# Norms of the queries: the two halves added on VectorE, and the exponential's table loaded earlier

## The chip, the core and the metric

The kernel runs on one core of one Trainium2 chip. The metric is the device time of one execution in microseconds (us); the median of several is taken. TensorE (PE), VectorE (DVE), ScalarE (ACT) and GpSimd (POOL) each work through a list of instructions of their own and wait for one another on semaphores; SyncE (SP) issues most of the transfers.

## What is computed

Four stages over x (8 batches of 256 tokens, width 256): a cross-attention to sets, a mixture of 16 experts with a shared one, a second cross-attention, and a second mixture of 8 experts. The change lies in the second cross-attention, of which this is the part that matters (with 256 image tokens only the image keys count):

```
x = x + L0_xattn(layernorm(x));  x = x + L0_ffn(layernorm(x))
def rms_norm(x, g, eps=1e-6):
    var = mean(x * x, axis=-1);  return x * rsqrt(var + eps) * g
q = rms_norm(layernorm(x) @ Wq + bq, gq)       # var: one number per token, over 256 columns
k_img = rms_norm(ctx_img @ Wk_img + bk_img, gk_img)
img_x = softmax(q k_img / 4) v_img             # 16 heads of 16 columns
x = x + img_x @ Wo + bo
x = x + L1_ffn(layernorm(x))
```

## The kernel before

The second cross-attention has two parts. In the first, the queries of all 8 batches are made; `queries(b)` and `squares(b)` are one batch of it. In the second, 16 tiles of 128 tokens (`NT`) go one by one through scores, maximum, exponential, transposition, values, division and projection.

Queries are kept transposed: the 256 columns of a query lie as two halves (`m` = 0, 1 of `KD` = 2) of 128 partitions, and the 256 tokens of a batch along the free axis. For each batch:

- PE, `queries(b)` (L1136): four fp32 matmuls 128x128 by 256 columns into one PSUM bank. In the trace each fp32 matmul is two records, so a batch is 8.
- ACT, `queries(b)` (L823, L825): for each half, a Square into `sqT` (in `arena`, two buffers and `sqT_last` for batch 7), then an Identity into `xnT`, which is the query itself; both add the bias. Semaphores `c_sq` and `c_qT` count them.
- PE, `squares(b)` (L1144): the squares are summed over the partitions, by matmuls of `sqT` with one column of ones. For each of the two tiles of a batch the halves `m` = 0 and 1 are accumulated in PSUM: four matmuls of one column, 8 records. `c_ssq` counts them, and ACT waits for it before it writes a buffer of `sqT` again.
- DVE, `mean_squares(half)` (L1620), for four batches at once, scales the sums; POOL raises them to -1/2 (L610, `rq`, semaphore `c_rq`), and the exponential takes `rq` as its scale.

The order on each engine is the order of the code. PE runs q0, the bias product of the output (L1157, L1158), the last piece of the first mixture's down projection, q1, s0, then q2, s1, q3, s2, q4, s3 (q for queries, s for squares), the transpositions of the normalised rows of batches 6 and 7 (L933, `turn_rows`), q5, s4, q6, s5, the scores of tile 0 (L1180), q7, s6, s7, the scores of tile 1, the transposition of tile 0's probabilities (L1189), values (L1202, L1209), and so on. The transposition of batch 7 takes its PSUM bank after ACT has copied batch 6 out of one (`copy_batch`, L711).

ACT runs q0, `bo_rows` (the output's bias, L829), q1 to q4, `preload_act_table(Exp)` (L832), the copies of batches 6 and 7, q5 to q7, and then the exponential of tile 0 (L846), which waits for `rq`, for tile 0's scores less their maximum (`c_shift`) and for s6.

DVE, after the first mixture, adds its last group to x (L1578), takes the statistics of batches 6 and 7 (L1384 to L1394) and their rows (`rows_of`, L1405), then `mean_squares(0)`, the maxima of tile 0 (L1626), its centring (L1634) and `mean_squares(1)`.

POOL meanwhile makes the block-diagonal keys (L588), adds the output's bias to x (L604, 8 instructions), and then makes `rq` (L610).

Of the kernel before, what the change touches and what calls it, by code (L numbers as in the profile page):

```python
# [14 lines left out]
ALU = mybir.AluOpType  # L15
ACT = mybir.ActivationFunctionType
AX = mybir.AxisListType

P = 128
B, S, D = 8, 256, 256  # L20
# [38 lines left out]
def program(nc, x_in, ctx_in, ctxT_in, itok_in, descT_in, wq0_in, bq0_in, rw0_in, ebias_in,  # L59
            gu0_in, dn0_in, wq1_in, bq1_in, gq1_in, wk1_in, bk1_in, gk1_in, wv1_in, bv1_in,  # L60
            wo1_in, bo1_in, wg1_in, wexp_in, out_rows):
    with ExitStack() as st:
# [3 lines left out]
        def sem(name):  # L66
            return st.enter_context(nc.semaphore(name))
# [35 lines left out]
        def view(tensor, first, *shape):  # L103
            v = tensor[:, first:first + int(np.prod(shape))]
            names = "abcd"[:len(shape)]
            if len(shape) > 1:
                v = v.rearrange(f"p ({' '.join(names)}) -> p {' '.join(names)}",
                                **dict(zip(names[:-1], shape)))
            return v
# [67 lines left out]
        sqT = view(arena, 1024, 2, KD, S)  # L177
        sqT_last = view(arena, 3072, KD, S)
        attT = view(wexp, last + 1280, 2, KD * P)
        rec1 = view(arena, 3840, P)  # L180
        attU = view(wexp, last + 1024, KD * P)
        srep1 = view(arena, 4096, P)
# [86 lines left out]
        def bank(i, n=1):  # L269
            return ps[:, 512 * i:512 * (i + n)]  # L270
# [22 lines left out]
        c_proj, c_pv, c_q, c_qT = sem("c_proj"), sem("c_pv"), sem("c_q"), sem("c_qT")  # L293
        c_rec, c_rq, c_scores = sem("c_rec"), sem("c_rq"), sem("c_scores")
        c_shift, c_sq, c_ssq, c_turned = sem("c_shift"), sem("c_sq"), sem("c_ssq"), sem("c_turned")
        c_var = sem("c_var")

        d_added, d_down, d_hT = sem("d_added"), sem("d_down"), sem("d_hT")
        d_hidden, d_logits, d_max, d_onehot = sem("d_hidden"), sem("d_logits"), sem("d_max"), sem("d_onehot")
# [52 lines left out]
        def each(eng, n, lead, step, body):  # L352


            for i in range(lead):
                body(i, i)
            with eng.Fori(0, (n - lead) // step) as turn:
                for j in range(step):
                    body(turn * step + (lead + j), lead + j)
# [347 lines left out]
        def _(act):  # L707
# [110 lines left out]
            def queries(b, k):  # L818
                act.wait_ge(c_q, b + 1)
                if k >= 2:  # L820
                    act.wait_ge(c_ssq, b - 1)
                for m in range(KD):
                    act.activation(sqT_last[:, m, :] if k == B - 1 else sqT[:, k % 2, m, :], bank(3 - k % 2)[:, m * S:(m + 1) * S], ACT.Square,  # L823
                                   bias=vecs[:, 0, m:m + 1]).then_inc(c_sq, 1)
                    act.activation(xnT[:, m, bass.ds(b * S, S)], bank(3 - k % 2)[:, m * S:(m + 1) * S],  # L825
                                   ACT.Identity, bias=vecs[:, 0, m:m + 1]).then_inc(c_qT, 1)
            queries(0, 0)
            act.wait_ge(bo_sum, 1)
            act.activation(bo_rows, bank(4)[:, 0:D], ACT.Copy).then_inc(bo_ready, 1)  # L829
            for b in range(1, 5):  # L830
                queries(b, b)
            act.preload_act_table(ACT.Exp)  # L832
            for b in range(B - 2, B):
                copy_batch(2, b, 0)
            for b in range(5, B):
# [83 lines left out]
        def _(pe):  # L919
# [218 lines left out]
                mm.then_inc(c_q, 1)  # L1138

            def squares(b, k):  # L1140
                pe.wait_ge(c_sq, b * KD + KD)
                for j in range(TB):
                    for m in range(KD):
                        mm = pe.matmul(bank(7 - b // 4)[:, b % 4 * TB + j:b % 4 * TB + j + 1], (sqT_last if k == B - 1 else sqT[:, k % 2])[:, m, j * P:(j + 1) * P],  # L1144
                                       ones[:, 0:1], start=(m == 0), stop=(m == KD - 1))
                mm.then_inc(c_ssq, 1)

            def queries_squares(b, k):
# [229 lines left out]
        def _(dve):  # L1378
# [18 lines left out]
            def rows_of(norm, b, k):  # L1397

                dve.wait_ge(ln_rstd, norm * B + b + 1)
                if k >= 2 or norm >= 2:  # L1400
                    dve.wait_ge(ln_turned, norm * B + b - 1)
                for j in range(TB):
                    t = b * TB + j
                    to = xn_of[norm]
                    r = dve.tensor_scalar(to[:, k % 2, j, :], x_sb[:, t, :], mean[:, bass.ds(t, 1)],  # L1405
                                          rstd[:, bass.ds(t, 1)], ALU.subtract, ALU.mult)
                r.then_inc(ln_rows, 1)
# [165 lines left out]
            def add_ffn0(g):  # L1573
                dve.wait_ge(b_down, g * C0 + C0)
                for j in range(2):
                    t = g * 4 + j * 2
                    o = x_sb[:, bass.ds(t, 2), :].rearrange("p t d -> p (t d)")
                    dve.tensor_tensor(o, o, bank(6 + j), ALU.add).then_inc(x_new, 1)  # L1578

            def ffn0_group(g, k):  # L1580
                if k:
                    add_ffn0(g - 1)
                for c in range(C0):
# [22 lines left out]
                    if k and c in (5, 7):  # L1606
                        rows_of(2, g * 2 - 2 + (c - 5) // 2, (c - 5) // 2)
            each(dve, NG, 1, 1, ffn0_group)
            add_ffn0(NG - 1)
            dve.wait_ge(x_new, XB)  # L1610
            for b in range(B - 2, B):
                stats(2, b)


            for b in range(B - 2, B):
                rows_of(2, b, b % 2)

            def mean_squares(half):
                dve.wait_ge(c_ssq, (half + 1) * B // 2)
                dve.tensor_scalar(ssq[:, half * NT // 2:(half + 1) * NT // 2], bank(7 - half)[:, 0:NT // 2], HD / D, HD * 1e-6,  # L1620
                                  ALU.mult, ALU.add).then_inc(c_var, 1)
# [33 lines left out]
            mean_squares(0)  # L1655
            maxima(0)
            centre(0)
            mean_squares(1)
            def stats_tile(j):
                t = NT - TB + j  # L1660
# [232 lines left out]
```

## Time and profile before

| | us |
|---|---|
| median of 3 runs | 766.83 (765.54 to 771.33) |
| the profiled execution | 766.84 |
| its span, first to last instruction | 765.1 |
| PE busy | 702.9 |
| DVE busy | 475.5 |
| POOL busy | 331.9 |
| ACT busy | 253.3 |

The profiled execution is as long as the median; 1.74 us of it lie outside the span. Times inside the span count from its start. "Busy" is an engine's own time, and PE's is modelled, since its matmuls overlap. The stretch that the change touches lies between 343 and 385 us.

### The profile page before, as it was taken

The numbers are of one execution on the slowest core, as the hardware profiler recorded it, in microseconds if no ns is written. First come the engines' busy times: TensorE is split into PE (matmuls) and PEld (weight loads), VectorE is DVE, ScalarE is ACT, GpSimd is POOL, SyncE is SP. The second block draws the span as 40 slices with busy tenths as digits, with TensorE's granted clock in tenths as the row PEclk, the third lists the DMA queues.
The fourth block names the chain that finished last, engine by engine and source line by source line (L and its number), as shares of the span: only waits on it lengthen the run. The fifth ranks groups of instructions, "written<-read, shape, count | busy, mean of one in ns | idle before, by whom it ended". The sixth has DMA issues, their size and how long they took to land.

```text
span 765.1 us, 14781 instructions
## 1 busy us (share of the span) xinstructions
PE 702.9 (92%) x4739; PEld 626.8 (82%) x4739; DVE 475.5 (62%) x1314; ACT 253.3 (33%) x474; POOL 331.9 (43%) x324
## 2 busy tenths in 40 slices
PE   4999569999999999998999994599999999999996
PEld 3858558878878888887777784599999999999995
DVE  5959956667767667763399968444554444454443
ACT  1356233222322232235456640122222222222221
POOL 6226943434334334436312125245554555365553
PEclk9997669999999999999899995699999999999998
DMA  9900136766667666747930008622345255435221
GB/s 218 327 2 17 40 118 212 237 220 223 201 222 239 225 206 217 246 159 324 431 100 29 30 30 280 218 36 44 73 116 155 46 160 158 147 55 148 43 37 22
DMA packets 60266, 114.97 MB, mean 150 GB/s; under 512 B 15185, under 2 KB 29394, under 8 KB 57778
## 3 DMA queue, kind: packets, MB, share of 16 engines
q1 hardware_dynamic: 50514, 103.48, 39.7%
q0 software_dynamic: 8736, 10.39, 8.4%
q8 instruction: 38, 0.62, 0.3%
q10 hardware_dynamic: 960, 0.33, 0.2%
q14 instruction: 18, 0.15, 0.1%
HBM read 68.89 MB, written 45.29 MB: 149 GB/s over the span
## 4 chain that ended last, share of the span: by engine, by line
PE 79%; DVE 13%; issue 4%; ACT 2%; DMA 1%; POOLq 0%; POOL 0%; DVEq 0%
PE ps L1061 18%; PE ps L1062 18%; PE ps L1063 18%; PE ps L1332 3%; PE ps L1180 2%; PE ps L1189 2%; PE ps L1136 2%; PE ps L1226 2%; PE ps L933 2%; PE ps L1104 1%; PE ps L988 1%; PE ps L1202 1%; PE ps L1311 1%; DVE h_low L1600 1%; DVE h_high L1596 1%
## 5 line engine op out<-in xcount | busy, mean ns | idle before, releaser
L574 POOL TENSOR_TENSOR part_lo<-wexp,part_hi 128x512 fp32r<-128x512 f32 x68 | 89.4, 1325 | 133.5 <-ACT part_hi L814 131.3
L681 POOL DMA_INDIRECT out_rows<-vbd,slot_row x39 | 63.3, 1624 | 107.4 <-DVE vbd L1808 73.4
L1061 PE MATMUL ps<-w_hi,x_high 128*128 x312 | 104.9, 336 | 1.1 <-DVE x_low L1813 1.1
L1063 PE MATMUL ps<-w_hi,x_low 128*128 x312 | 101.5, 325 | 0.0
L1062 PE MATMUL ps<-up_low,x_high 128*128 x312 | 101.5, 325 | 0.0
L1829 DVE TENSOR_TENSOR arena<-arena,ps 128x704 f32<-128x704 f32 x39 | 34.6, 888 | 100.4 <-ACT arena L901 81.2
L1061 PE MATMUL ps<-xn_high,gu_high 128*128 (+3 forms) x208 | 92.6, 445 | 0.2
L803 ACT ACTIVATE wexp<-ps 128x512 f32<-128x512 f32 (+1 forms) x52 | 31.1, 598 | 160.3 <-PE ps L1063 160.3
L1062 PE MATMUL ps<-xn_low,gu_high 128*128 (+3 forms) x208 | 82.3, 396 | 0.0
L1063 PE MATMUL ps<-xn_high,gu_low 128*128 (+3 forms) x208 | 82.2, 395 | 0.0
L514 POOL TENSOR_TENSOR rstd<-ve,mhalf 128x2 f32<-128x2 f32 (+1 forms) x31 | 22.2, 716 | 110.2 <-DVE ve L1394 110.2
L901 ACT ACTIVATE arena<-ps 128x704 f32<-128x704 f32 x39 | 29.6, 759 | 119.9 <-PE ps L1063 81.0
L1061 PE MATMUL ps<-dn_high,h_high 128*128 128x256 f32 (+1 forms) x208 | 61.3, 295 | 5.4 <-DVE h_low L1600 5.4
L1061 PEld LDWEIGHTS ps<-w_hi,x_high 128*128 128x128 f32 x312 | 59.7, 191 | 1.5 <-issue 1.5
L1061 PE MATMUL ps<-w_hi,hT_high 128*128 x195 | 59.0, 302 | 2.0 <-DVE hT_high L1822 2.0
L1062 PEld LDWEIGHTS ps<-up_low,x_high 128*128 128x128 f32 x312 | 59.7, 191 | 0.0
L1586 DVE TENSOR_TENSOR wexp<-wexp,ps 128x512 f32<-128x512 f32 (+1 forms) x52 | 35.7, 686 | 38.5 <-ACT wexp L803 38.4
L1063 PEld LDWEIGHTS ps<-w_hi,x_low 128*128 128x128 f32 x312 | 59.4, 191 | 0.0
L1062 PE MATMUL ps<-dn_low,h_high 128*128 128x256 f32 (+1 forms) x208 | 58.8, 283 | 0.0
L1063 PE MATMUL ps<-dn_high,h_low 128*128 128x256 f32 (+1 forms) x208 | 58.6, 282 | 0.0
L1600 DVE TENSOR_TENSOR h_low<-wexp,h_high 128x256 fp32r<-128x256 f32 (+1 forms) x104 | 55.4, 574 | 1.8
L1063 PE MATMUL ps<-w_hi,hT_low 128*128 x195 | 55.7, 286 | 0.0
(286 smaller groups left out, 1701.5 us busy)
## 6 DMA issues: line engine op xcount, KB each, us to landing
wexp<-in_wexp SPq DMA_DIRECT2D x68, 256.0 KB, 3.2
w_hi_rows<-part_hi SPq DMA_DIRECT2D x68, 256.0 KB, 2.7
w_lo_rows<-part_lo SPq DMA_DIRECT2D x68, 256.0 KB, 2.0
w_hi<-w_hi_rows SPq DMA_DIRECT2D x8, 2048.0 KB, 19.6
up_low<-w_lo_rows SPq DMA_DIRECT2D x8, 1408.0 KB, 6.0
down_low<-w_lo_rows SPq DMA_DIRECT2D x8, 768.0 KB, 8.6
wexp<-in_gu SPq DMA_DIRECT2D x2, 1632.0 KB, 10.8
xn_rows<-arena SPq DMA_DIRECT2D x8, 256.0 KB, 2.1
```

Source lines behind the costliest of these rows:

```text
L514: pool.tensor_tensor(rstd[:, bass.ds(b * TB, TB)], ve[:, bass.ds(b * TB, TB)], mhalf[:, 0:1].broadcast_to([P, TB]), ALU.pow).then_inc(ln_r ...
L574: pool.tensor_tensor(part_lo[:, n % 2, :], part_w[:, n % 4, :], part_hi[:, n % 2, :].bitcast(F32), ALU.subtract).then_inc(p_lo, 1)
L681: pool.indirect_dma_start(out=out_rows, out_offset=bass.IndirectOffsetOnAxis(ap=slot_row[:, i:i + 1], axis=0), in_=yb[:, i % 2, :], in_off ...
L803: act.activation(sg0[0:rows, c % 2, :], bank(c % 2)[0:rows, :], ACT.Silu).then_inc(b_silu, 1)
L901: act.activation(sg1.rearrange("p (a n) -> p a n", a=2), bank(0, 2).rearrange("p (a n) -> p a n", a=2)[:, :, 0:HALF1], ACT.Silu).then_inc( ...
L1061: pe.matmul(out, high, rows_high, start=start, stop=False, skip_group_check=True)
L1062: pe.matmul(out, high, rows_low, start=False, stop=False, skip_group_check=True)
L1063: return pe.matmul(out, low, rows_high, start=False, stop=stop, skip_group_check=True)
L1332: mm = pe.transpose(bank(4, 2)[:, c * P:(c + 1) * P], h1[:, c * P:(c + 1) * P], ident[:, :])
L1586: dve.tensor_tensor(hm0[0:rows_, c % 2, :], sg0[0:rows_, c % 2, :], bank(2 + c % 2)[0:rows_, :], ALU.mult).then_inc(b_prod, 1)
L1600: dve.tensor_tensor(h_low[0:rows_, c % 2, cols], hm0[0:rows_, c % 2, cols], h_high[0:rows_, c % 2, cols].bitcast(F32), ALU.subtract).then_ ...
L1829: dve.tensor_tensor(h1[:, 0:I1].rearrange("p (a n) -> p a n", a=2), sg1.rearrange("p (a n) -> p a n", a=2), bank(2, 2).rearrange("p (a n) ...
```

## The change

`squares_of(b)` names the buffer of a batch's squares. ACT now makes both Squares of a batch first and both Identities after them. A new DVE instruction for each batch, `sum_squares(b)`, adds half 1 to half 0 in place (128x256, fp32) and counts `sq_sum`; PE's `squares(b)` waits for that and needs one matmul for each tile in place of two. The table of the exponential is loaded behind `bo_rows` in place of behind q4.

```
-                    act.activation(sqT_last[:, m, :] if k == B - 1 else sqT[:, k % 2, m, :], bank(3 - k % 2)[:, m * S:(m + 1) * S], ACT.Square,
+                    act.activation(squares_of(k)[:, m, :], bank(3 - k % 2)[:, m * S:(m + 1) * S], ACT.Square,
                                    bias=vecs[:, 0, m:m + 1]).then_inc(c_sq, 1)
+                for m in range(KD):
                     act.activation(xnT[:, m, bass.ds(b * S, S)], bank(3 - k % 2)[:, m * S:(m + 1) * S],
                                    ACT.Identity, bias=vecs[:, 0, m:m + 1]).then_inc(c_qT, 1)
             queries(0, 0)
             act.wait_ge(bo_sum, 1)
             act.activation(bo_rows, bank(4)[:, 0:D], ACT.Copy).then_inc(bo_ready, 1)
+            act.preload_act_table(ACT.Exp)
             for b in range(1, 5):
                 queries(b, b)
-            act.preload_act_table(ACT.Exp)
...
             def squares(b, k):
-                pe.wait_ge(c_sq, b * KD + KD)
+                pe.wait_ge(sq_sum, b + 1)
                 for j in range(TB):
-                    for m in range(KD):
-                        mm = pe.matmul(bank(7 - b // 4)[:, b % 4 * TB + j:b % 4 * TB + j + 1], (sqT_last if k == B - 1 else sqT[:, k % 2])[:, m, j * P:(j + 1) * P],
-                                       ones[:, 0:1], start=(m == 0), stop=(m == KD - 1))
+                    mm = pe.matmul(bank(7 - b // 4)[:, b % 4 * TB + j:b % 4 * TB + j + 1], squares_of(k)[:, 0, j * P:(j + 1) * P],
+                                   ones[:, 0:1], start=True, stop=True)
                 mm.then_inc(c_ssq, 1)
...
+            def sum_squares(b):
+                dve.wait_ge(c_sq, b * KD + KD)
+                to = squares_of(b)
+                dve.tensor_tensor(to[:, 0, :], to[:, 0, :], to[:, 1, :], ALU.add).then_inc(sq_sum, 1)
+            sum_squares(0)
             add_ffn0(NG - 1)
             dve.wait_ge(x_new, XB)
             for b in range(B - 2, B):
                 stats(2, b)
-
-
+            sum_squares(1)
             for b in range(B - 2, B):
                 rows_of(2, b, b % 2)
+            for b in range(2, B - 1):
+                sum_squares(b)
...
             maxima(0)
             centre(0)
+            sum_squares(B - 1)
             mean_squares(1)
```

What stands on DVE between the statistics of batch 7 and the maxima of tile 1, before (L1405 are the rows of batches 6 and 7, L1620 `mean_squares`, L1626 the maxima, L1634 the centring):

```order
L1394 TENSOR_SCALAR ve<-mv 128x2
L1405 TENSOR_SCALAR arena<-x_sb,mean,rstd 128x256 [waits ln_turned,ln_rstd]
L1405 TENSOR_SCALAR arena<-x_sb,mean,rstd 128x256
L1405 TENSOR_SCALAR arena<-x_sb,mean,rstd 128x256 [waits ln_turned,ln_rstd]
L1405 TENSOR_SCALAR arena<-x_sb,mean,rstd 128x256
L1620 TENSOR_SCALAR ssq<-ps 128x8 [waits c_ssq]
L1626 TENSOR_REDUCE mx<-ps 128x16 [waits c_scores]
L1634 TENSOR_TENSOR arena<-ps,mx 128x1024 [waits c_max]
L1620 TENSOR_SCALAR ssq<-ps 128x8 [waits c_ssq]
```

The same place in the changed kernel, whose line numbers are some lines higher (L1408 for L1405, L1630 for L1620, L1636 for L1626, L1644 for L1634; L1616 is `sum_squares`):

```order
L1397 TENSOR_SCALAR ve<-mv 128x2
L1616 TENSOR_TENSOR arena<-arena 128x256 [waits c_sq]
L1408 TENSOR_SCALAR arena<-x_sb,mean,rstd 128x256 [waits ln_turned,ln_rstd]
L1408 TENSOR_SCALAR arena<-x_sb,mean,rstd 128x256
L1408 TENSOR_SCALAR arena<-x_sb,mean,rstd 128x256 [waits ln_turned,ln_rstd]
L1408 TENSOR_SCALAR arena<-x_sb,mean,rstd 128x256
L1616 TENSOR_TENSOR arena<-arena 128x256 [waits c_sq] x5
L1630 TENSOR_SCALAR ssq<-ps 128x8 [waits c_ssq]
L1636 TENSOR_REDUCE mx<-ps 128x16 [waits c_scores]
L1644 TENSOR_TENSOR arena<-ps,mx 128x1024 [waits c_max]
L1616 TENSOR_TENSOR arena<-arena 128x256 [waits c_sq]
L1630 TENSOR_SCALAR ssq<-ps 128x8 [waits c_ssq]
```

One sum stands ahead of the rows of batches 6 and 7, five ahead of `mean_squares(0)` and the maxima of tile 0, and one behind tile 0's centring; the sum of batch 0 stands ahead of the stretch shown.

On ACT, from the output's bias to the copies of batches 6 and 7, q1 and q4 shown of the four batches between, before:

```order
L829 ACTIVATE wexp<-ps 128x256 [waits bo_sum]
L823 ACTIVATE arena<-ps,vecs 128x256 [waits c_q]
L825 ACTIVATE xmem<-ps,vecs 128x256
L823 ACTIVATE arena<-ps,vecs 128x256
L825 ACTIVATE xmem<-ps,vecs 128x256
...
L832 ACT_TABLE_LOAD
L711 ACTIVATE xmem<-ps 128x2x256 [waits ln_turned] x2
```

and in the changed kernel (L833 is the output's bias, L826 Square, L829 Identity, L714 the copies):

```order
L833 ACTIVATE wexp<-ps 128x256 [waits bo_sum]
L834 ACT_TABLE_LOAD
L826 ACTIVATE arena<-ps,vecs 128x256 [waits c_q]
L826 ACTIVATE arena<-ps,vecs 128x256
L829 ACTIVATE xmem<-ps,vecs 128x256 x2
...
L714 ACTIVATE xmem<-ps 128x2x256 [waits ln_turned] x2
```

The load has moved ahead of q1, and in every batch the second Square stands ahead of the first Identity. PE's order is as before, with two matmuls in each `squares` where there were four.

## Rows read from the trace of the kernel before

**Rows 1.** The page: granted TensorE clock in forty slices, in tenths.

```profile
PEclk9997669999999999999899995699999999999998
```

**Rows 2.** Chain of waits from 343 to 374 us: start, duration, engine, tile and line.

```profile
350.26 0.79 PE ps L1144 x8
351.05 1.83 PE ps L1136 x8
...
361.04 0.61 ACT xmem L711
```

**Rows 3.** Timeline of TensorE: start, duration; in brackets idle time before and what ended it.

```profile
361.78 0.63 PE L933 MATMUL ps<-ident,arena 128*128 128x128 f32 x4 [2.38 <-ACT xmem L711]
...
368.54 1.99 PE L1136 MATMUL ps<-xmem,wq 128*128 128x256 f32 x8
...
371.83 1.05 PE L1144 MATMUL ps<-ones,arena 128*128 128x1 f32 x8 [0.51 <-ACT arena L823]
...
374.02 1.97 PE L1189 MATMUL ps<-ident,arena 128*128 128x128 f32 x8
377.10 1.08 PE L1202 MATMUL ps<-wexp,vbd 128*32 128x128 f32 x16 [1.11 <-ACT wexp L852]
...
378.96 1.87 PE L1180 MATMUL ps<-wexp,xmem 64*128 64x256 f32 x8
...
382.97 0.65 PE L1202 MATMUL ps<-wexp,vbd 128*32 128x128 f32 x16 [0.67 <-ACT wexp L852]
...
384.04 1.14 PE L1180 MATMUL ps<-wexp,xmem 64*128 64x256 f32 x8
385.13 1.09 PE L1189 MATMUL ps<-ident,arena 128*128 128x128 f32 x8
```

**Rows 4.** Timeline of ScalarE, the same columns.

```profile
346.94 0.38 ACT L829 ACTIVATE wexp<-ps 128x256 f32<-128x256 f32 x1
350.30 0.47 ACT L823 ACTIVATE arena<-ps,vecs 128x256 f32<-128x256 f32 x1 [2.97 <-PE ps L1136]
...
358.16 0.47 ACT L823 ACTIVATE arena<-ps,vecs 128x256 f32<-128x256 f32 x1 [1.05 <-PE ps L1136]
...
359.24 0.48 ACT L825 ACTIVATE xmem<-ps,vecs 128x256 f32<-128x256 f32 x1
359.75 1.28 ACT L832 ACT_TABLE_LOAD   x1
```

**Rows 5.** One line of VectorE (L1600): ns min/median/max, first and last start.

```profile
L1600 DVE TENSOR_TENSOR h_low<-wexp,h_high x104: 411/422/1506, 108.1 to 345.2; 128x256 fp32r<-128x256 f32 x96, 96x256 fp32r<-96x256 f32 x8
```

**Rows 6.** Timeline of VectorE from 348 to 371 us.

```profile
348.57 1.28 DVE L1578 TENSOR_TENSOR x_sb<-x_sb,ps 128x512 f32<-128x512 f32 x2 [2.90 <-PE ps L1063]
...
352.33 0.73 DVE L1405 TENSOR_SCALAR arena<-x_sb,mean,rstd 128x256 f32<-128x256 f32 x2
353.33 1.32 DVE L1405 TENSOR_SCALAR arena<-x_sb,mean,rstd 128x256 f32<-128x256 f32 x2 [0.27 <-POOL rstd L514]
...
369.91 1.23 DVE L1634 TENSOR_TENSOR arena<-ps,mx 128x1024 f32<-128x1024 f32 x1
```

**Rows 7.** Timeline of GpSimd from 353 to 367 us.

```profile
353.27 2.42 POOL L588 TENSOR_TENSOR wexp<-kT,gmask 128x256 f32<-128x256 f32 x4
355.65 9.84 POOL L604 TENSOR_TENSOR x_sb<-x_sb,wexp 128x512 f32 x8
365.45 1.64 POOL L610 TENSOR_TENSOR rq<-ssq,mhalf 128x8 f32<-128x8 f32 x1
```

**Rows 8.** Timelines of GpSimd and VectorE around 84 us.

```profile
83.63 1.83 POOL L532 TENSOR_TENSOR gu_low<-wexp,gu_high 128x768 fp32r<-128x768 f32 x1
...
84.26 1.48 DVE L1542 TENSOR_TENSOR arena<-arena,ebias 128x256 f32<-128x256 f32 x1
```

**Rows 9.** Stretches: busy time (count) by engine, then PEclk, DMA share, GB/s.

```profile
373.00:374.00 1.00, 1.00 (x8) 0.50 (x6) 0.08 (x1) 0.32 (x1) 0.84 (x1) 0.84 0.88 377
374.00:380.00 6.00, 4.89 (x48) 3.79 (x48) 3.35 (x3) 2.44 (x3) 1.95 (x3) 0.50 1.00 429
```

More of the change, by code:

```diff
@@ L179, in program, with squares_of @@
         attT = view(wexp, last + 1280, 2, KD * P)
+        def squares_of(b):
+            return sqT_last if b == B - 1 else sqT[:, b % 2, :, :]
         rec1 = view(arena, 3840, P)
@@ L295, in program @@
         c_shift, c_sq, c_ssq, c_turned = sem("c_shift"), sem("c_sq"), sem("c_ssq"), sem("c_turned")
-        c_var = sem("c_var")
+        c_var, sq_sum = sem("c_var"), sem("sq_sum")
         d_added, d_down, d_hT = sem("d_added"), sem("d_down"), sem("d_hT")
```

## The prediction

> **What bounds the kernel now.** I read the page first: TensorE is busy for 702.9 of 765.1 us, and its clock is granted in full except in a few stretches [rows 1]. So time is won only where PE itself gets less work or waits less. The chain of waits, taken from 343 to 374 us, shows that the queries' part is PE's own: a `squares` of 0.79 us and a `queries` of 1.83 us in turn, five times, with one break [rows 2]. The timeline of TensorE names the break: 2.38 us of idle time ahead of the transposition of batch 7 at 361.78, ended by ACT's copy of batch 6 [rows 3]. The timeline of ScalarE tells why that copy was late: ACT was through with q4 at 359.24 + 0.48 = 359.72, loaded the table for 1.28 us, and only then copied [rows 2, 4]. A second, smaller wait stands ahead of s7, 0.51 us for ACT's last Square [rows 3]. After s7 come the scores of tile 1 and the transposition of tile 0's probabilities at 374.02, and from there the tiles run as they did; what is won by that point is what the kernel wins, but for the clock.
>
> **The table.** It now stands behind `bo_rows`, which ends at 346.94 + 0.38 = 347.32. ACT then had nothing for 2.97 us, until q1 at 350.30 [rows 4]. The load needs 1.28 of them and costs nothing there; if that gap went, q1's activations would be late by at most 1.28. Behind q4 it is gone, so the copy of batch 6 can start 1.28 us sooner, and next late is still ACT (q4's four activations end 1.6 us after q4's matmuls, s3 and batch 6's transposition are done before). **Gain: 1.28.** The Square and Identity of q5 to q7 already ran on this table before, so no second load follows. As to the load's price, the row shows the next activation 0.01 us after the load's end [rows 2, 4]. The Trainium skill (ScalarE: Activation LUTs, What ACT_TABLE_LOAD costs) adds a drain of some 1.38 us to every switch; by that rule the move would be worth about 2.66 us, called an estimate from that page. The rows have no such gap, so they speak against it.
>
> **The matmuls.** Each `squares` falls from 8 records to 4, from 0.79 to about 0.40 us: 0.39 less, 8 times [rows 2]. Not all of it is on the path. s0, s1 and s2 are, since ACT's q4 follows them. s3 is not: it lies in the wait that ACT sets. s4 and s5 are. s6 is not, because PE then waits for s7 anyway. **Gain: 5 x 0.39 = 1.95.**
>
> **s7** stands alone. Before, it began 371.83 - 370.53 = 1.30 us after q7's end and lasted 1.05 [rows 3]. Now the second Square ends at 0.02 + 0.36 + 0.47 = 0.85 after q7 (the four activations of a batch start 0.36 apart, 358.16 to 359.24 in three steps [rows 4]), the sum takes 0.42 [rows 5], and with a hand-over of 0.04 the start is at 1.31. So the wait stays the same, and the matmuls give 0.39. **Gain: 0.38.** The sum of batch 7 is queued behind tile 0's centring on DVE, which before ended at 369.91 + 1.23 = 371.14, 0.6 us after q7 [rows 6], and goes along with the scores of tile 0; it is ready in time. Behind this sum wait only `mean_squares(1)` and the maxima of tile 1, whose scores come later still.
>
> Without any new wait that is 1.28 + 1.95 + 0.38 = **3.61 us**.
>
> **The sums on DVE.** No instruction of this form stands in this stretch. Its nearest row is the 128x256 tensor_tensor from SBUF to SBUF, 0.42 us at the median and 1.51 at most [rows 5]. Why so far apart is shown around 84 us: a 128x256 tensor_tensor begun at 84.26 took 1.48 us and ended at 85.74, 0.28 after the POOL instruction beside it (83.63 + 1.83 = 85.46) [rows 8]. So a sum that meets a running POOL instruction ends some 0.3 us after it. The Trainium skill (SBUF — State Buffer, SBUF: two separate sides) has the rule: DVE with two SBUF inputs and GpSimd exclude each other, for a whole instruction. The trace agrees, by those two rows [rows 8]. And POOL is at work from 353.27 to 367.09 without a break: four of 0.61, eight of 1.23, and `rq` [rows 7]. A sum needs 0.42 to 0.3 + 1.23 = 1.53 us there. I walk the batches, with s(b) due 1.83 after the end of q(b), and the Squares done at 0.85:
> - Sum 0 finds DVE idle for the 2.90 us before 348.57 [rows 6] and is hidden; it would cost if the down projection ended 2.4 us sooner.
> - Sum 1 stands behind the statistics and starts at 352.33, where the rows of batch 6 did [rows 6]; it ends at 352.75. PE is through q2 at 350.26 + 0.40 + 1.83 = 352.49 and can go on at about 352.80: **0.31 lost**.
> - Sum 2 stands behind the rows of batch 7, which ended at 354.65 [rows 6] and now some 0.25 later, and then behind the last POOL instruction but one of the keys, to about 355.4; PE is ready at 353.20 + 1.83 = 355.03: **0.4 lost**.
> - Sum 3: Squares at 355.9, POOL's instruction ends near 356.9, the sum near 357.2; PE is ready at 357.7. Nothing lost.
> - Sum 4 lies under the break for batches 6 and 7, sum 6 under the scores of tile 0 and q7. Nothing lost.
> - Sum 5: ready near 363.3, held to 364.4, done at 364.7; PE is ready at 364.6: **0.1 lost**.
>
> The loss is 0.8, between 0 and 4 x (0.85 + 1.53 + 0.04 - 1.83) = 2.4 us (all four exposed sums held for a whole instruction). I take 0.8, from the walk.
>
> **Other queues.** Five sums stand ahead of `mean_squares(0)`, so `rq` can start only after sum 6, near 366.2, or when POOL is through with the bias at 365.5. The exponential of tile 0 is not ready before 369.7, so 367.9 for `rq` is soon enough. If instead POOL is held 0.42 by each of five sums, the bias ends at 367.6 and `rq` at 369.2: still in time, with 0.5 to spare. SP's loads and PE's queue pass nothing.
>
> **The sum.** 3.61 - 0.83 = 2.8 us, from the profiled execution of 766.84 us (which is the median within 0.01): **764.0 us**.
>
> **The clock.** From late in the microsecond ahead of 374, and through 380, the granted clock is 0.50, the lower level of 1.2 GHz [rows 9]. Before it fell, PE had a stretch of one-column matmuls, a wait of 0.51 us, and the scores of tile 1. At that level the transposition took 1.97 in place of 1.09, values 1.86 (377.10 to 378.96) in place of 1.07, scores 1.80 in place of 1.09: 2.4 us lost [rows 3]. The change makes the thin stretch between q7 and the first values shorter, from 6.6 to about 5.1 us. The rows don't tell whether that is enough.
>
> **Rivals.**
> 1. *The clock does not fall.* As the forecast, and 2.4 more: 766.84 - 2.8 - 2.4 = 761.6 us. For it: the slice with the wait of 2.38 us (the nineteenth) had the clock in full [rows 1, 3]. Against: the fall came in a stretch that stays thin.
> 2. *The sums are late nearly everywhere.* PE's saving turns into waits for DVE behind POOL: 3.61 - 2.4 = 1.2, so 765.6 us. For it: 1.51 us at most in [rows 5] and a POOL without a break. Against: DVE is idle otherwise and three of the sums are covered.
> 3. *Slower: PE's new waits bring the clock down a second time.* Waits for `sq_sum` of 0.4 to 0.6 us after each thin `squares`, in the stretch from 352 to 366 us, and a second half-clock stretch about as long as the first [rows 9], 7 us of busy PE: 3.5 us lost. With rival 2's waits, 766.84 - 1.2 + 3.5 = 769.1 us. It decides from a loss of more than 2.8 us beyond the walk's. Against: the wait of 2.38 us did not do it before.
> 4. *The change does not do what it says*, for instance a second table load before the exponential on ACT: the gain of 1.28 goes, 765.3 us. The order of instructions shows one load at that place and none later.
>
> **How the numbers follow.** Forecast 764.0 (762.6 to 765.2 with its own bounds): 0.45. Rival 1: 0.30. Rival 2: 0.14. Rival 3: 0.05. Rival 4: 0.02; the rest, 0.04, is something unseen. The range has to reach from rival 1, with its sum without any loss (760.7), to rival 2 and the little that two executions differ (766.9); that leaves out rival 3 and a part of the rest. A measurement of this kernel tells no change from one of under 1%, 7.7 us. Faster by that would need more than all gains together (3.61 + 2.4 = 6.0): 0.03. Slower by that: 0.01. Within it: 0.96.
>
> **What would show it.** The load in ACT's gap near 347.4; an idle time of about 1.1 to 1.5 us in place of 2.38 before batch 7's transposition; `squares` of 4 records and 0.4 us; s1 and s2 with waits of 0.3 to 0.4 us for DVE; sums between 0.42 and 1.5 us; tile 0's transposition starting near 371.0. Wrong would be the forecast if sums 3 and 5 are waited for, if the exponential waits for POOL's `rq`, or if the clock goes another way.

## The result, and the profile after

The changed kernel takes 760.29 us (median of 20 executions, 757.62 to 765.01), the one before 767.05 us (20 executions beside them, 764.91 to 773.23). The ratio is 0.9916, with a 95% interval of 0.9898 to 0.9934: 6.4 us faster (5.1 to 7.8). Forecast were 764.0 us and 2.8 us of gain, in a range whose lower end, 760.7, lies just above the measured time. The profiled execution took 759.37 us, 7.5 less than that of before, with a span of 757.6 us.

The page's row of the granted clock, to be held against [rows 1], has a full twentieth digit, where before had an 8. The digit alone proves little, since a slice is 19 us long: three traces further below have a fall of the clock in this stretch and a 9 in the twentieth place all the same (before's third, the changed kernel's second and fifth).

```profile
PEclk9997569999999999999999995699999999999998
```

The timeline of TensorE (start, duration, in brackets idle time and what ended it) answers to [rows 2, 3]:

```profile
346.76 1.89 PE L1140 MATMUL ps<-xmem,wq 128*128 128x256 f32 x8
348.49 0.50 PE L1147 MATMUL ps<-ones,arena 128*128 128x1 f32 x4
348.85 1.97 PE L1140 MATMUL ps<-xmem,wq 128*128 128x256 f32 x8
351.20 0.61 PE L1147 MATMUL ps<-ones,arena 128*128 128x1 f32 x4 [0.38 <-DVE arena L1616]
351.67 1.97 PE L1140 MATMUL ps<-xmem,wq 128*128 128x256 f32 x8
353.86 0.60 PE L1147 MATMUL ps<-ones,arena 128*128 128x1 f32 x4 [0.21 <-DVE arena L1616]
354.32 1.97 PE L1140 MATMUL ps<-xmem,wq 128*128 128x256 f32 x8
...
358.53 0.63 PE L937 MATMUL ps<-ident,arena 128*128 128x128 f32 x4 [1.40 <-ACT xmem L714]
359.00 1.89 PE L1140 MATMUL ps<-xmem,wq 128*128 128x256 f32 x8
...
364.39 1.99 PE L1140 MATMUL ps<-xmem,wq 128*128 128x256 f32 x8
366.23 0.50 PE L1147 MATMUL ps<-ones,arena 128*128 128x1 f32 x4
367.77 0.60 PE L1147 MATMUL ps<-ones,arena 128*128 128x1 f32 x4 [1.05 <-DVE arena L1616]
368.31 1.14 PE L1183 MATMUL ps<-wexp,xmem 64*128 64x256 f32 x8
369.38 1.09 PE L1192 MATMUL ps<-ident,arena 128*128 128x128 f32 x8
371.58 0.65 PE L1205 MATMUL ps<-wexp,vbd 128*32 128x128 f32 x16 [1.11 <-ACT wexp L856]
...
376.94 1.14 PE L1183 MATMUL ps<-wexp,xmem 64*128 64x256 f32 x8
```

The wait ahead of batch 7's transposition is 1.40 us where it was 2.38; two new ones of 0.38 and 0.21 us stand ahead of s1 and s2, for sums on DVE; that ahead of s7 is 1.05 us where it was 0.51, but s7 itself has half the work. And the transposition of tile 0's probabilities takes 1.09 us where it took 1.97 in [rows 3]: here the clock has not fallen.

ScalarE loads the table in the gap before q1, and the next activation starts 1.68 us after the load's end:

```profile
345.73 1.28 ACT L834 ACT_TABLE_LOAD   x1
348.69 0.84 ACT L826 ACTIVATE arena<-ps,vecs 128x256 f32<-128x256 f32 x2 [1.67 <-PE ps L1140]
```

VectorE's sums, for [rows 5, 6]: 0.42 us at best, 0.48 to 1.23 us beside POOL's running instructions (sums 1, 2 and 3 shown):

```profile
350.73 0.42 DVE L1616 TENSOR_TENSOR arena<-arena 128x256 f32<-128x256 f32 x1
...
352.97 0.83 DVE L1616 TENSOR_TENSOR arena<-arena 128x256 f32<-128x256 f32 x1
354.55 1.23 DVE L1616 TENSOR_TENSOR arena<-arena 128x256 f32<-128x256 f32 x1 [0.75 <-ACT arena L826]
```

GpSimd, for [rows 7]: its eight instructions of the bias took 10.39 us in place of 9.84, and `rq` then waited 0.44 us for DVE, without harm:

```profile
354.23 10.39 POOL L607 TENSOR_TENSOR x_sb<-x_sb,wexp 128x512 f32 x8
365.07 1.65 POOL L613 TENSOR_TENSOR rq<-ssq,mhalf 128x8 f32<-128x8 f32 x1 [0.44 <-DVE ssq L1630]
```

**Where the pair of traces differs.** I cut each execution at two starts of TensorE's timeline: q1 (348.37 before, 346.76 after) and the scores of tile 3 (384.04 [rows 3], 376.94 after). The head is 1.61 us shorter, the middle 35.67 before and 30.18 after (5.49 shorter), the tail 381.06 and 380.66. Of the change, the head holds only batch 0's activations, its sum and the load, and from q0's start to q1's it is 4.84 us in both traces; so its 1.61 us are not the change's. The pair alone tells less than it seems to, and more traces were wanted.

### The profile page after: what moved, and what is told of

The parts are those of the page before. It is cut to its first block, busy times and chain, and to the rows that moved or that the text cites. A ratio compares the mean times of both kernels' runs of the same rounds, so it can differ in the third digit from the quotient of the medians.

```text
span 757.6 us, 14725 instructions
## 1 busy us (share of the span) xinstructions
PE 697.8 (92%) x4707; PEld 622.5 (82%) x4707; DVE 480.2 (63%) x1322; ACT 253.1 (33%) x474; POOL 332.3 (44%) x324
## 3 DMA queue, kind: packets, MB, share of 16 engines
q0 software_dynamic: 8736, 10.39, 8.4%
## 4 chain that ended last, share of the span: by engine, by line
PE 78%; DVE 14%; issue 4%; ACT 2%; DMA 1%; POOLq 0%; POOL 0%; DVEq 0%
PE ps L1065 19%; PE ps L1066 18%; PE ps L1067 18%; PE ps L1335 3%; PE ps L1192 2%; PE ps L1183 2%; PE ps L1229 2%; PE ps L1108 1%; PE ps L937 1%; PE ps L1314 1%; PE ps L1205 1%; DVE h_high L1599 1%; DVE h_low L1603 1%; PE ps L1140 1%; PE ps L1221 1%
```

## The experiments

Theory A: some 3 us are work off PE's path, the rest is the granted clock, which falls in thin stretches of PE's work in a part of the executions, and less often with the change. Theory B: the path is all that the change does, and the clock is the draw of an execution. Times are ratios to the kernel before, run beside each on the same chip, with 95% intervals; traces are read by the cut above. A middle is called clean when the granted clock is 1.00 all through it. Each run's short name stands in brackets.

**The table load alone** (table_only). Before, with

```
             act.activation(bo_rows, bank(4)[:, 0:D], ACT.Copy).then_inc(bo_ready, 1)
+            act.preload_act_table(ACT.Exp)
             for b in range(1, 5):
                 queries(b, b)
-            act.preload_act_table(ACT.Exp)
```

> The kernel before with the table load alone moved behind the output's bias. Theory A (the gain of 6.4 to 6.8 us is work taken off PE's path, some 3 us, plus a half-clock stretch behind q7 that the shorter thin stretch avoids, 2.4 us): the load's 1.28 us come off the wait ahead of batch 7's transposition (2.38 to about 1.1 us), the stretch from s6 to the first values stays as thin as before and the clock still falls there in the profile, so about 1.3 us faster than before, ratio 0.998. Theory B (the clock's part is the draw of an execution and has nothing to do with the change): the same 1.3 us, and the clock at that place now so, now so. A third possibility, that the table load was worth more than its own duration (a drain, as the page has it): 2.6 us.

Measured: 0.9959 (0.9935 to 0.9982), 3.1 us faster (1.4 to 5.0). TensorE's timeline:

```profile
360.05 0.63 PE L933 MATMUL ps<-ident,arena 128*128 128x128 f32 x4 [0.96 <-ACT xmem L711]
```

The wait fell from 2.38 to 0.96 us: 1.42, which is the load and 0.14 us of hand-over that went with it. The middle was 31.64 us, and clean. That is against theory A's forecast for this trace: the stretch behind q7 was as thin as before, and the clock did not fall in it. The load is no more than 1.42 us on the path, so the drain that the Trainium skill adds to a load (ScalarE: Activation LUTs, What ACT_TABLE_LOAD costs) is not seen here. The interval of the ratio just reaches down to 1.4 us, so the run does not prove that anything beyond the load was won.

**The sums alone** (sums_only). The changed kernel, with the load back behind q4:

```
             act.activation(bo_rows, bank(4)[:, 0:D], ACT.Copy).then_inc(bo_ready, 1)
-            act.preload_act_table(ACT.Exp)
             for b in range(1, 5):
                 queries(b, b)
+            act.preload_act_table(ACT.Exp)
```

> The changed kernel with the table load back behind q4, so the sums on VectorE alone. Theory A: 1.75 us off the path (3.03 measured in the pair of traces less 1.28), and the clock stays in full behind q7, 2.4 us more: 4.2 us faster than before, ratio 0.9945. Theory B: 1.75 us, ratio 0.998.

Measured: 0.9965 (0.9938 to 0.9992), 2.7 us faster (0.6 to 4.8), which tells neither theory from the other. The trace had what neither had foreseen. First TensorE's timeline, then the stretches (busy time by engine, granted clock, DMA share, GB/s):

```profile
363.49 0.63 PE L937 MATMUL ps<-ident,arena 128*128 128x128 f32 x4 [2.83 <-ACT xmem L714]
363.95 3.20 PE L1140 MATMUL ps<-xmem,wq 128*128 128x256 f32 x8
366.94 0.85 PE L1147 MATMUL ps<-ones,arena 128*128 128x1 f32 x4
```

```profile
358.00:364.00 6.00, 3.17 (x21) 2.76 (x22) 2.45 (x2) 4.23 (x9) 6.00 (x5) 1.00 1.01 434
364.00:368.00 4.00, 4.00 (x15) 3.41 (x14) 0.00 (x0) 1.41 (x4) 3.97 (x4) 0.57 1.01 430
```

Behind a wait of 2.83 us the clock fell to the lower level: q5 took 3.20 us where it takes 1.89. Behind q7 it stayed full. So there is a second place for a fall, 1.6 us dear (q5's start to q6's is 3.70 us here, 2.09 in the changed kernel), and the first trace of before had only happened not to show it. The gain of the sums on the path is 33.07 - (33.28 - 1.61) = 1.4 us (33.28 is this trace's middle; 33.07 is the middle of before with the clock full, worked out below).

**Before, with dense work in the thin stretch** (before_dense). Three fp32 matmuls of 256 columns round s7, into a PSUM bank that nothing reads then:

```
+            def dense(n):
+                for i in range(n):
+                    pe.matmul(bank(4)[:, 0:S], wq1[:, 0, 0:P], xnT[:, 0, 0:S], start=True, stop=True)
             scores(0, 0)
             queries_squares(B - 1, B - 1)
+            dense(1)
             squares(B - 1, B - 1)
+            dense(2)
```

> The kernel before, with three more fp32 matmuls of 256 columns in the thin stretch, one in PE's wait ahead of s7 and two behind s7; they write a PSUM bank that nobody reads then. Their direct cost is 0.9 us (two of 0.46 on the path). Theory A: the thin stretch is no longer thin, the clock stays in full behind it, 2.4 us back: 1.5 us faster than before, ratio 0.998. Theory B: 0.9 us slower, ratio 1.001, and the clock at that place as often low as before.

Measured: 0.9954 (0.9929 to 0.9980): 3.5 us faster (1.5 to 5.4) with more work. The stretches:

```profile
359.00:362.00 3.00, 0.62 (x6) 0.41 (x5) 0.12 (x1) 2.62 (x5) 3.00 (x4) 1.00 0.97 410
362.00:366.00 4.00, 4.00 (x16) 3.31 (x15) 0.00 (x0) 0.91 (x2) 4.00 (x4) 0.57 1.02 438
366.00:384.00 18.00, 16.22 (x160) 13.12 (x159) 8.80 (x9) 9.02 (x18) 3.90 (x4) 1.00 1.01 432
```

Behind q7 (from 372.2 us here) the clock stayed full, behind the untouched wait of 2.38 us it fell. Theory B, which wanted 0.9 us more, is out by the ratio; only matmuls were added, and one of the three fills PE's wait. By the trace alone nothing was gained: its middle is 35.72 us, since it has the other fall.

**Before, dense at both places** (before_dense_both). The same, and

```
             for b in range(B - 2, B):
-                turn_rows(2, b, b % 2)
+            turn_rows(2, B - 2, 0)
+            dense(4)
+            turn_rows(2, B - 1, 1)
```

> The run before_dense with four more matmuls of 256 columns (1.8 us) in PE's wait of 2.38 us ahead of the transposition of batch 7, where they cost nothing. Theory A, widened by the last runs (the clock falls at two places, behind that wait, 1.6 us, and behind q7, 2.4 us, in a part of the executions): neither can fall, so faster than before_dense by its share of the first fall, at most 1.6 us; against before 2 to 4 us faster, although the path is 0.9 us longer. Theory B (what the dense matmuls gave was chance): 0.9 us slower than before.

Measured: 0.9948 (0.9928 to 0.9967), 4.0 us faster than before (2.5 to 5.5). The whole stretch has the clock full:

```profile
357.00:390.00 33.00, 30.57 (x282) 24.89 (x284) 16.05 (x19) 18.26 (x30) 13.77 (x13) 1.00 0.97 379
```

Its middle is 34.03 us, 0.96 above the clean 33.07. So theory B is out: the matmuls that were added cost 0.96 us on the path, and several times as much came back. Not all of it came back in this stretch: this execution also kept its clock at a third place near the end of the kernel (below), where nothing was changed.

**The changed kernel, made thinner** (after_thin). s7's matmuls four times:

```
-                for j in range(TB):
+                for j in list(range(TB)) * (4 if b == B - 1 else 1):
```

> The changed kernel with the one-column matmuls of s7 made four times, which makes the thin stretch 1.1 to 1.2 us longer (as long as before). Theory A: the clock falls there again, 1.1 plus 2.4 us: 3.5 us slower than the changed kernel, about 3.1 us faster than before, ratio 0.996. Theory B: 1.1 us slower than the changed kernel, ratio to before 0.993.

Measured: 0.9968 (0.9945 to 0.9992), 2.5 us faster than before, so 4.0 us slower than the changed kernel by the two ratios (with an uncertainty of some 2.3), for 1.1 to 1.2 us of added work. Timeline, and one stretch:

```profile
369.36 2.79 PE L1147 MATMUL ps<-ones,arena 128*128 128x1 f32 x16 [1.05 <-DVE arena L1616]
372.08 2.08 PE L1183 MATMUL ps<-wexp,xmem 64*128 64x256 f32 x8
```

```profile
370.00:380.00 10.00, 8.89 (x64) 7.04 (x65) 3.45 (x4) 3.20 (x4) 2.81 (x3) 0.51 1.00 426
```

The low stretch already takes in the repeated matmuls (2.79 us for 16 records), and the middle is 35.73 us, 5.55 above the changed kernel's clean one. More thin work before tile 0's scores brought the fall, as theory A has it; this is one trace, and the ratio agrees with it.

**The changed kernel, dense in its waits** (after_dense). Two dense matmuls in each of the waits of 1.40 and 1.05 us, which costs the path nothing:

```
-            for b in range(B - 2, B):
-                turn_rows(2, b, b % 2)
...
+            turn_rows(2, B - 2, 0)
+            dense(2)
+            turn_rows(2, B - 1, 1)
...
             queries_squares(B - 1, B - 1)
+            dense(2)
             squares(B - 1, B - 1)
```

> The changed kernel with two dense matmuls of 256 columns in each of PE's two waits (1.40 us ahead of batch 7's transposition, 1.05 us ahead of s7), 0.9 us each, so without cost on the path. Theory A: the changed kernel keeps its clock at both places in most executions already, so little or nothing is gained, under 1 us, and its slow third of executions (near 764.4) gets rarer if that is a fall at these places. Theory C (the slow third is a fall somewhere else, the waits have no part in it): the same time and the same spread as the changed kernel.

Measured: 0.9901 (0.9881 to 0.9921), 759.86 us median of 5, none above 760.55. Against the changed kernel (0.9914, next but one) that is no difference that can be told. Its middle, 30.19, is clean. Against before_dense_both, whose middle is clean too, it is 0.9901 to 0.9948, 3.6 us less: the two paths differ by 34.03 - 30.19 = 3.84, of which 0.96 is before_dense_both's own added work. So the path alone is 2.9 us by clean traces on both sides, and the ratios agree within their uncertainty of some 2 us.

**The order on ScalarE alone** (order_only). Before, with both Squares ahead of both Identities:

```
                     act.activation(sqT_last[:, m, :] if k == B - 1 else sqT[:, k % 2, m, :], bank(3 - k % 2)[:, m * S:(m + 1) * S], ACT.Square,
                                    bias=vecs[:, 0, m:m + 1]).then_inc(c_sq, 1)
+                for m in range(KD):
                     act.activation(xnT[:, m, bass.ds(b * S, S)], bank(3 - k % 2)[:, m * S:(m + 1) * S],
```

> The kernel before with both Squares of a batch ahead of both Identities on ScalarE, and nothing else. The last Square of batch 7 ends 0.37 us sooner, so s7 starts 0.37 us sooner (wait of 0.14 in place of 0.51 us) and nothing else moves: 0.4 us faster on the path, ratio within the noise of 1.000 (0.9975 to 1.0015).

Measured: 1.0006 (0.9982 to 1.0030), as expected. In the trace s6 and s7 now stand in one row, with no wait between them that is long enough to be listed:

```profile
373.72 2.15 PE L1145 MATMUL ps<-ones,arena 128*128 128x1 f32 x16
375.79 1.13 PE L1181 MATMUL ps<-wexp,xmem 64*128 64x256 f32 x8
```

From q7 (371.89) to the scores of tile 1 it is 3.90 us where before had 4.27, and 3.92 in the changed kernel: for batch 7 the order does all that there is, and the sum on DVE adds and takes nothing. The clock fell behind the wait of 2.38 us (q5's start to q6's 4.22 us, where it is 2.54 at full clock); without that, the middle of 34.38 us would be 32.70, the forecast 0.4 below 33.07.

**The changed kernel again**, unchanged.

> The changed kernel unchanged, beside the others on the same chip, and for a second trace. Theory A: 6.4 us faster than before again; path from q1 to the transposition of tile 0 22.6 us, and the granted clock full there in most executions, the low stretches elsewhere shifted against the first trace by the draw. Theory B (the first trace's full clock was the draw): the clock falls behind q7 in this one.

Measured: 0.9914 (0.9883 to 0.9945). This time the clock did fall behind q7, in a shorter stretch:

```profile
358.00:369.00 11.00, 8.64 (x52) 7.34 (x50) 5.34 (x7) 6.70 (x18) 9.58 (x8) 1.00 1.01 430
369.00:374.00 5.00, 4.32 (x20) 3.15 (x20) 2.57 (x4) 2.01 (x3) 2.82 (x3) 0.66 1.02 436
```

Middle 31.81 us, so 1.6 lost. The change does not rule the fall out, and a full clock "in most executions" was not borne out: the traces below show the fall in three of five.

**Sums placed earlier.**

```
             for b in range(B - 2, B):
                 stats(2, b)
-            sum_squares(1)
-            for b in range(B - 2, B):
-                rows_of(2, b, b % 2)
-            for b in range(2, B - 1):
+                if b == B - 2:
+                    sum_squares(1)
+            rows_of(2, B - 2, 0)
+            sum_squares(2)
+            rows_of(2, B - 1, 1)
+            for b in range(3, B - 1):
                 sum_squares(b)
```

> The changed kernel with two sums placed earlier on VectorE: the sum of batch 1 between the statistics of batches 6 and 7, the sum of batch 2 between their rows. The two waits of PE for sums in the changed kernel's trace (0.38 us ahead of s1, 0.21 ahead of s2) go: path 0.5 to 0.6 us shorter than the changed kernel, ratio to before 0.990 to 0.992. Rival: VectorE then meets GpSimd's keys with the rows of batch 7, or the sum of batch 2 is held behind them, and PE waits as before: no difference.

Measured: 0.9894 (0.9851 to 0.9937), not to be told from the changed kernel, but the trace is clear: no wait ahead of s1 and s2, and q1's start to q4's takes 6.44 us where it took 7.56. In this draw the clock fell behind q7 (middle 31.77).

**The same, dense in the waits** (that order with after_dense's matmuls).

> The last run's order, and the dense matmuls of after_dense in PE's two remaining waits. Theory A: path 0.6 us shorter than after_dense and the clock in full at both places: fastest of all, ratio to before 0.989 to 0.991. Rival: no difference to after_dense that can be told.

Measured: 0.9894 (0.9866 to 0.9922), with the shortest middle of all, 29.13 us, clock full:

```profile
350.06 1.89 PE L1140 MATMUL ps<-xmem,wq 128*128 128x256 f32 x8
...
352.15 1.97 PE L1140 MATMUL ps<-xmem,wq 128*128 128x256 f32 x8
...
354.32 1.97 PE L1140 MATMUL ps<-xmem,wq 128*128 128x256 f32 x8
...
356.50 1.97 PE L1140 MATMUL ps<-xmem,wq 128*128 128x256 f32 x8
```

q2, q3 and q4 stand 2.17 and 2.18 us apart, in the changed kernel 2.82 and 2.65. The waits of 0.38 and 0.21 us thus cost 0.65 and 0.47, each some 0.26 more than its idle time. In the rows, a `squares` that follows its `queries` at once starts 0.16 us before the end recorded for them and takes 0.50 us; behind a wait it starts after that end and takes 0.61. This version beats both kernels' paths (by 1.05 and 3.9 us); in the ratio it can be told from before, not from the changed kernel. What can be told is the spread. None of the eleven executions with dense matmuls in both waits (this run and after_dense) took more than 761.22 us, while nine of the changed kernel's 26 timed executions took more than 761.5. Of its five traces, the three with a fall took 762.65 to 765.51 us, the two without 757.86 and 759.37. So its slow third belongs to falls in this stretch, at least in part, and theory C (a fall somewhere else) is unlikely.

**Six more traces**, to count falls: the kernel before three times, the changed one three times.

> The kernel before once more, for its trace alone. Theory A: the clock falls in it at one or both of the two places, behind the wait ahead of batch 7's transposition (costs 1.6 us) or behind q7 (2.4 us), by the draw of the execution. Theory B (the clock cannot explain more than the 2.4 us of the first trace): it falls behind q7 only.

> The same as the run before it, a further draw: under theory A another mixture of the two places, under theory B behind q7 only.

> The changed kernel once more, for its trace alone. Theory A: the clean middle (q1 to the scores of tile 3) is 30.2 us; where the clock falls behind q7 it is 1.6 to 2.6 us longer; never does it fall behind the wait ahead of batch 7's transposition, now 1.40 us. Theory C: the slow third of its executions (near 764.4) has a clean middle and is long elsewhere.

> As the run before it, a further draw: middle 30.2 us, or 31.8 to 32.8 with a fall behind q7; none behind the wait ahead of batch 7's transposition.

> As the two runs before it, a further draw, with the same numbers: middle 30.2 us, or 31.8 to 32.8 with a fall behind q7.

> The kernel before, a further draw: clean middle 33.2 us, and one or both falls on top (1.4 to 1.6 us, 2.5 us); a clean middle would speak for the draw's having a larger part.

Before's second trace fell at both places and its third behind the wait alone, so theory B's forecast (behind q7 only) failed in both; the changed kernel's three came out as theory A had them. The stretches of before's second trace:

```profile
357.00:360.00 3.00, 0.75 (x7) 0.51 (x6) 0.17 (x1) 2.96 (x5) 3.00 (x3) 1.00 1.01 426
360.00:364.00 4.00, 3.87 (x12) 3.27 (x13) 0.00 (x0) 0.60 (x1) 4.00 (x5) 0.57 1.02 438
364.00:374.00 10.00, 9.49 (x66) 8.20 (x65) 2.62 (x3) 5.86 (x13) 2.22 (x2) 1.00 1.00 428
374.00:381.00 7.00, 5.89 (x49) 4.18 (x50) 3.45 (x4) 2.44 (x3) 1.97 (x3) 0.51 1.01 431
```

All traces of the two kernels, cut at q1 and at the scores of tile 3 (us):

| trace | time | head | middle | tail | clock fell |
|---|---|---|---|---|---|
| before | 766.84 | 348.37 | 35.67 | 381.06 | behind q7 |
| before, 2nd | 766.95 | 346.72 | 37.40 | 381.08 | at both |
| before, 3rd | 765.72 | 348.44 | 34.74 | 380.82 | behind the wait |
| before, 4th | 766.16 | 348.01 | 35.67 | 380.52 | behind q7 |
| changed | 759.37 | 346.76 | 30.18 | 380.66 | - |
| changed, 2nd | 762.96 | 348.08 | 31.81 | 381.31 | behind q7 |
| changed, 3rd | 765.51 | 349.83 | 32.79 | 381.18 | behind q7 |
| changed, 4th | 757.86 | 347.34 | 30.18 | 378.58 | - |
| changed, 5th | 762.65 | 348.24 | 31.79 | 380.87 | behind q7 |

The clean middle of the changed kernel is 30.18, twice over. That of before never came clean; by its steps it is 30.18 + 2.89 = 33.07 (next section). The 34.74 of its 3rd trace, less the 1.68 us lost behind the wait, gives 33.06, and so does table_only's clean 31.64 with its 1.42 us added. Falls cost before 2.60, 4.33, 1.67 and 2.60 us, 2.8 on the mean; the changed kernel 0, 1.63, 2.61, 0 and 1.61, 1.2 on the mean. None of the changed kernel's five lay behind the wait of 1.40 us. The dearest of them, 765.51, has a late head and a fall, the cheapest, 757.86, neither of them and a short tail.

The two places differ in what the change does to them, and here all traces on record can be counted. Behind PE's wait ahead of batch 7's transposition the clock fell in five of seven traces with a wait of 2.38 or 2.83 us (before four times, before_dense, order_only, sums_only), and in none of seven with a wait of 1.40 (the changed kernel five times, after_thin, the sums placed earlier). Behind q7 it fell in three of six traces with before's `squares` (before, table_only, order_only) and in four of seven with the changed ones (the changed kernel, sums_only, the sums placed earlier); in none of four with dense matmuls there, and in after_thin's. So the changed kernel keeps its clock at the first place. That it keeps it more often behind q7, as theory A has it, is not shown; what dense and thin work do there is.

**A third place, near the end.** Ahead of the kernel's last matmuls PE waits 2.00 us for DVE, in every trace. In fourteen of the eighteen traces the clock falls behind this wait, and PE's last stretch takes 3.6 to 3.8 us; in four (the changed kernel's 4th, sums_only, before_dense_both, after_dense) it stays full, the stretch takes 2.3 us, and the tail is 378.1 to 378.6 us where all others have 380.1 to 381.4. A part of that stretch in before, then in before_dense_both:

```profile
756.00:758.00 2.00, 2.00 (x9) 2.00 (x10) 0.01 (x1) 0.00 (x0) 0.00 (x0) 0.50 0.56 66
```

```profile
752.00:754.00 2.00, 1.39 (x11) 1.40 (x12) 0.63 (x4) 0.00 (x0) 0.24 (x1) 1.00 0.57 66
```

No edit touches this place. Whether an edit 370 us earlier has a part in what the clock does there, or only chance, the traces do not tell.

## Why the prediction was wrong

The path was forecast as 2.8 us, and the traces give 2.89. The step that failed is **"The clock"**: the sum puts the clock's part at nothing, since it takes the fall behind q7 as the only one and as staying where it is. It also held the slice with the wait of 2.38 us [rows 1, 3] for evidence that such a wait does no harm, in rival 1 and again in rival 3. The runs showed in its place that the clock falls behind that very wait in five of seven traces, for 1.6 to 1.7 us each, and never behind the 1.40 us that the change leaves. Over the traces of the two kernels falls cost 2.8 us on the mean before and 1.2 after, so 1.6 us of gain stood outside the sum. By the ratio, all that lies beyond the path is 6.4 - 2.9 = 3.5 us, 2.2 to 4.9; where the rest of it lies is only partly known (end of this section).

Point by point:
- *The table: 1.28.* Measured 1.42 (table_only: wait 2.38 to 0.96; in the changed kernel q4's start to q5's 6.10 to 4.68). Hidden in ACT's gap as said. The drain that the Trainium skill adds to a load (ScalarE: Activation LUTs, What ACT_TABLE_LOAD costs) was rightly left out.
- *The matmuls: 5 x 0.39.* Measured 0.45 for each batch (q5 to q6 2.54 before, 2.09 after; q6 to q7 3.75 and 3.30; q1 to q2 2.54 and 2.09), 2.25 for five. I had halved the 0.79 us of the chain, but from s0's start to q2's it is 0.81 us with eight records and 0.36 with four: less than half is left.
- *s7: 0.38.* Measured 0.35 (q7 to the scores of tile 1, 4.27 to 3.92).
- *The sums' waits: 0.3 + 0.4 + 0.1.* Measured 0.38, 0.21 and none, in PE's time 0.65 + 0.47 = 1.12, against the 0.83 of the sum: two of the three places are right, and each wait costs 0.26 us more than its idle time.
- These add up: 1.42 + 2.25 + 0.35 - 1.12 = 2.90, or step by step from q1 to the scores of tile 1, 2.89. That the sum of 2.8 came so near is in part luck: three of its terms are off by 0.14, 0.30 and 0.29 us, and the errors cancel.
- *Sum 3, `rq`, the queue on POOL*: as said. Sum 3 took 1.23 us and nobody waited; the exponential took `rq` 1.3 us after it was ready; POOL's eight instructions, beside which four sums ran, became 0.55 us longer in ten, not by the 0.42 for each sum that I had as the bad end.
- *Rivals.* Rival 1 names the mechanism and a time of 761.6 us, 1.3 above the measured one, but it knows one place only, and there the clock still falls in three of the changed kernel's five traces. Rival 2 had the right kind of loss and twice its size (2.4, measured 1.12). Rivals 3 and 4 are refuted: behind the waits for sums the clock fell in no trace, and the load stands where it should.
- *The bounds.* 766.84 - 3.61 - 2.4 is 760.8, not 760.7, and a loss of 0 to 2.4 us gives 763.2 to 765.6 for the forecast's own bounds, not 762.6 to 765.2. What matters more: both start from one execution and its one fall. The median of the changed kernel is not one path from one execution, for heads differ by up to 3.1 us and tails by 2.7 between traces of the same kernel.
- *What a measurement can tell.* I had put the limit at 1%. With twenty executions of each kernel the interval is 0.9898 to 0.9934, so a change of 0.84% is told clearly.

What stays open: by the traces, four against five, the means differ by 2.9 of path, 1.6 of falls, 0.35 of tail and -0.2 of head, 4.7 us in all, and the ratio says 5.1 to 7.8. Most of what lies between is a matter of which executions were traced: before's four average 766.4 us and its twenty timed ones 767.5, the changed kernel's five 761.7 and its twenty 761.2. Nine of before's twenty took 767.8 to 773.2 us, and no trace shows one of those. What is long in them is not known. The 4.0 us of before_dense_both ask for nothing more: its trace is 4.4 us below the mean of before's four, 1.8 in the middle, 2.8 in the tail (the third place) and -0.2 in the head.

## What to carry to other kernels

A wait on TensorE can cost more than its idle time: price it with the clock that it may bring down behind it, at every place, and read several traces before you say that a place keeps its clock. Be wary of matmuls of one column beside short waits: the clock fell behind such a stretch too, and it fell there again when more of them were added. Where a wait cannot be taken away, dense matmuls that fit into it cost the path nothing, and in the three kernels here that had them at both places the clock stayed full through the stretch.

## What the runs showed of the hardware that I had not expected

- The granted clock fell to the lower level behind a wait of 2.38 us in some executions (before, 2nd and 3rd trace) and not in others (1st and 4th), by the same program; behind a wait of 1.40 us in none of seven. Behind the wait of 2.00 us near the end it fell in fourteen traces of eighteen. Behind the stretch from q7 to tile 0's first values, which has two runs of one-column matmuls and waits of 0.5 to 1.1 us, it fell although PE was never idle for longer than 1.11 us.
- Work that was added made the kernel faster: by 4.0 us (2.5 to 5.5) for seven matmuls that nobody needs.
- The head differs between executions by up to 3.1 us. Part of that is eight matmuls of 512 columns near 40 us, which took 6.48 us in the first trace of before and 4.92 in that of the changed kernel, with a granted clock of 1.00 in both records. In the changed kernel's 3rd trace the record says 0.50 there up to 44.9 us, and they took 5.99 us, so in the head the recorded clock does not explain the durations.
- A DVE instruction gets its turn among POOL's that stand back to back, and POOL loses little: 0.55 us over eight instructions (9.84 to 10.39) with four sums among them, which themselves took 0.48 to 1.23 us in place of 0.42.
